# A running maximum taken in four chunks, transposes in one pass, and small operations moved between engines, in a fused adaLN, mLSTM and mixture-of-experts kernel

## The chip, the cores and the metric

The kernel runs on one core of a Trainium2 chip. The metric is the device time of one execution in microseconds, and several executions give a median. A second source is one profiled execution of the kernel, with a record for each instruction. The engines are TensorE (PE; PEld are its weight loads), VectorE (DVE), ScalarE (ACT), GpSimd (POOL) and SyncE (SP), which issues most transfers. All data is float32; fp32r is a float32 that TensorE multiplies in one pass.

## What is computed

For each of 8 rows of 512 tokens with 128 features: a layer norm with shift and scale from a small condition vector, an mLSTM block, a gated residual, a second layer norm, and a mixture of 8 experts with the best 2 of them.

```python
h = _layernorm(x) * (1 + ca) + sa
normed = h * rsqrt(mean(h * h) + 1e-6) * norm_w        # rms norm
q, k, v, zi, zf, o = projections of normed             # o through a sigmoid
# one step for each of the 512 tokens
m_t = maximum(zf_t + m, zi_t)
i_p = exp(zi_t - m_t);  f_p = exp(zf_t + m - m_t)
C_t = f_p * C + i_p * outer(v_t, k_t);  n_t = f_p * n + i_p * k_t
h_t = o_t * (C_t @ q_t) / maximum(abs(sum(n_t * q_t)), 1.0)
# then
x = x + ga * (h + h_t @ Wout.T)
h = _layernorm(x) * (1 + cb) + sb
gate = softmax over the best two of h @ Wr + br
x = x + gb * sum_e gate_e * (relu(h @ W1_e + b1_e) @ W2_e + b2_e)
```

The recurrence is computed for all tokens of a row at once. With F the running sum of zf and a = zi − F, the maximum of the recurrence is m_t = F_t + M_t with M the running maximum of a over the tokens. The weight of token s in the output of token t is exp(a_s − M_t) for s up to t, times the score k_s · q_t. So the kernel needs M along the tokens, and it needs it in every partition, since the weights stand with s on the partitions and t along the free dimension.

## The kernel before

A row of 512 tokens is NT = 4 tiles of P = 128 tokens. The code of each engine is one function, `body`, called for b = −2 to 7, in steps t = 3 to 18. A call, a *turn*, interleaves three rows. Row b is in its expert part: there are N = 16 steps, half an expert each. Row b + 1 ends its mLSTM part (`end`): output product, residual, second layer norm, logits, gates. Row b + 2 begins (`start`): first norm, projections, running sum and maximum, weights, products with v. The first turn (b = −2) has no expert part and no ending row. In the second (b = −1, `opening`) the expert part begins at step 16. From b = 0 to 5 all three rows are present. The turns for b = 6 and 7 have no starting row.

In an expert step t, PE makes three products of 512 columns for the first layer (L1109 to L1111: high part times high part and the two cross terms), and three for the second layer of step t − 3 (L1125, L1126, L1135). Between them DVE applies bias, relu and gate (hg, L852), ACT rounds to the high part (hg_hi, L521), and DVE or POOL subtracts to get the low part (hg_lo). `POOL_STEPS` says which steps are POOL's (L468): 1 and 8 to 15. The other low parts are DVE's (L865). The last product of step t − 3 waits for the low part. After its six products PE runs `chain(b, end, start, t)`, the small products of the other two rows. DVE has `middle(t)` ahead of a possible low part and `after(t)` behind it.

The order on every engine is written out by hand. Each engine takes its instructions in that order, and semaphores make it wait for the others. SP writes the gates of a row to DRAM and reads them back, spread over the partitions (gate_bc), and its queue goes in order too. The first hg of the next row waits for that transfer.

The steps that the change touches, in a turn with b from 0 to 5:

- Step 8: POOL takes rms from ms_eps by a power (L456), behind four operations of the second norm. Step 9: DVE waits for it and makes rms2, its square (L749), rms_inv, its reciprocal (L750), and copies rms to the last column of vs (L751). Then it makes zo, zg, the running sum zp (L806) and vs.
- Step 11: DVE makes a_col, 128 tokens on the partitions by 4 tiles (L816).
- Step 12: PE turns the four columns into one row of 512, four transposes into one partition (L1013), and makes the scores of tile 0 (L949, L950). DVE takes top_d and max_index for the gates of row b + 1 (L730, L732), and then the running maximum m_row over the 512 elements of the one partition (L820).
- Step 13: PE spreads m_row over 128 partitions, as ones times m_row, a full float32 product of two passes with one row of the array (L1024). DVE runs the chain to the gates (L737 to L785), then makes mb, the spread maximum with the triangle mask (L823).
- Step 14: PE transposes the gates (L1146), ACT copies them to gate_rows (L563), and SP writes them out. PE's first product of step 15 waits for gate_rows. Steps 14 to 16: ACT makes the weights ew from mb and a_col (L498, L500), DVE multiplies them with the scores (L700). Step 18: PE multiplies them with vs (L1039), and DVE makes the denominator den from rms_inv (L890) and uh.

## Time and profile before

| | us |
|---|---|
| median of 3 runs | 338.03 |
| lowest and highest | 336.07, 340.14 |
| the profiled execution | 336.87 |
| its span, first instruction to last | 335.0 |
| mean granted clock of PE | 0.995 |

The profiled execution's time is 1.87 us above its span. A turn is read as the distance from one L961 to the next. Durations are of that one execution. Products of PE are pipelined: the duration of one overlaps the next, so what one costs in PE's order is the distance from its start to the next start. "Idle before" in brackets is the time that the engine waited ahead of an instruction, with the instruction that released it.

### The profile page before, as it was taken

Reading aid. Unit: us, or ns where it says so; the run is one execution under the profiler, and the core shown is the slowest. Engines: PE = TensorE matmul, PEld = TensorE weight load, DVE = VectorE, ACT = ScalarE, POOL = GpSimd, SP = SyncE. Lnnn points to the kernel's source line nnn. Section 1 sums busy time; section 2 is a strip of 40 time slices with the busy share of each in tenths; the row PEclk is TensorE's granted clock in tenths of the full one; section 3 lists DMA queues with packets and bytes.
Section 4 is the critical chain, followed back from the end, with each engine's and each line's share of the span. In section 5 each row is a group of like instructions: output and inputs, shape, how many; then the busy total and the mean of one; then the engine's idle time right before and its main releaser. Section 6 shows DMA issues by size and latency. Waiting matters only on the chain.

```text
span 335.0 us, 5104 instructions
## 1 busy us (share of the span) xinstructions
PE 323.0 (96%) x1767; PEld 258.4 (77%) x1767; DVE 280.8 (84%) x800; ACT 165.7 (49%) x303; POOL 171.1 (51%) x173
## 2 busy tenths in 40 slices
PE   7989989999999999999999999999999989999996
PEld 7769756887787868786888778786878668777995
DVE  6796696999699987999699969998779958887874
ACT  1542426555546554563755564754547363346542
POOL 6440550588427853487347842785408832435440
PEclk9999999999999999999999999999999997999999
DMA  4770004100250006100520025000610034004201
GB/s 132 243 203 0 2 0 153 72 1 0 81 204 3 0 6 249 31 1 2 201 85 0 0 78 210 0 2 2 250 34 0 0 115 171 1 1 179 75 2 31
DMA packets 13456, 23.62 MB, mean 71 GB/s; under 512 B 1764, under 2 KB 8087, under 8 KB 12407
## 3 DMA queue, kind: packets, MB, share of 16 engines
q1 hardware_dynamic: 13202, 23.17, 20.4%
q8 instruction: 14, 0.23, 0.3%
q14 instruction: 12, 0.09, 0.1%
q10 hardware_dynamic: 164, 0.07, 0.1%
q0 software_dynamic: 64, 0.07, 0.1%
HBM read 21.07 MB, written 2.23 MB: 70 GB/s over the span
## 4 chain that ended last, share of the span: by engine, by line
PE 78%; DVE 8%; DMA 5%; POOL 3%; ACT 2%; issue 2%; SPq 1%; DVEq 0%; POOLq 0%
PE bank L1109 9%; PE bank L1125 8%; PE bank L1111 8%; PE bank L1110 8%; PE bank L1135 8%; PE bank L1126 8%; PE bank L1039 6%; PE bank L1024 3%; PE bank L972 3%; DMA gate_bc<-gates_d 2%; DMA br_bc<-in_L_ffn_br_dram 2%; PE bank L1154 2%; PE bank L987 2%; PE bank L1146 1%; PE bank L1160 1%
## 5 line engine op out<-in xcount | busy, mean ns | idle before, releaser
L468 POOL TENSOR_TENSOR hg_lo<-hg,hg_hi 128x512 fp32r<-128x512 f32 x65 | 87.7, 1358 | 73.7 <-ACT hg_hi L521 73.7
L521 ACT ACTIVATE hg_hi<-hg 128x512 fp32r<-128x512 f32 x128 | 79.8, 628 | 77.9 <-DVE hg L852 76.7
L852 DVE SCALAR_TENSOR_TENSOR hg<-bank,neg_b,gate_bc 128x512 f32<-128x512 f32 x128 | 94.2, 741 | 25.1 <-DMA gate_bc<-gates_d 14.0
L1109 PE MATMUL bank<-h_hi,w_hi 128*128 128x512 f32 x128 | 58.5, 457 | 1.5 <-ACT gate_rows L563 1.5
L1125 PE MATMUL bank<-hg_hi,w_hi 128*128 128x512 f32 (+1 forms) x144 | 53.8, 374 | 0.0
L1135 PE MATMUL bank<-hg_lo,w_hi 128*128 128x512 f32 (+1 forms) x144 | 53.4, 371 | 0.0
L1126 PE MATMUL bank<-hg_hi,w_lo 128*128 128x512 f32 (+1 forms) x144 | 53.1, 369 | 0.0
L1111 PE MATMUL bank<-h_lo,w_hi 128*128 128x512 f32 x128 | 50.8, 397 | 0.0
L1110 PE MATMUL bank<-h_hi,w_lo 128*128 128x512 f32 x128 | 50.7, 396 | 0.0
L865 DVE TENSOR_TENSOR hg_lo<-hg,hg_hi 128x512 fp32r<-128x512 f32 x63 | 47.4, 752 | 1.1 <-ACT hg_hi L521 0.6
L437 POOL TENSOR_SCALAR var_eps<-mv 128x4 f32<-128x4 f32 x16 | 4.0, 251 | 66.7 <-DVE mv L598 66.7
L1109 PEld LDWEIGHTS bank<-h_hi,w_hi 128*128 128x128 f32 x128 | 24.3, 190 | 12.5 <-DVE hg L852 8.9
L1126 PEld LDWEIGHTS bank<-hg_hi,w_lo 128*128 128x128 f32 x144 | 27.3, 190 | 5.5
L1125 PEld LDWEIGHTS bank<-hg_hi,w_hi 128*128 128x128 f32 x144 | 27.2, 189 | 5.6
L1135 PEld LDWEIGHTS bank<-hg_lo,w_hi 128*128 128x128 f32 x144 | 27.1, 188 | 5.5 <-DVE hg_lo L865 0.3
L1111 PEld LDWEIGHTS bank<-h_lo,w_hi 128*128 128x128 f32 x128 | 24.2, 189 | 5.8
L1110 PEld LDWEIGHTS bank<-h_hi,w_lo 128*128 128x128 f32 x128 | 24.4, 191 | 3.6 <-issue 1.4
L1039 PEld LDWEIGHTS bank<-vs,ew 128*128 128x128 f32 x160 | 18.6, 193 | 3.3 <-DVE ew L700 3.2
L700 DVE TENSOR_TENSOR ew<-ew,bank 128x512 f32<-128x512 f32 (+3 forms) x32 | 14.8, 482 | 7.0 <-ACT ew L500 6.7
L1039 PE MATMUL bank<-vs,ew 128*128 128x65 f32 x160 | 19.5, 277 | 1.2 <-DVE ew L700 1.1
L447 POOL TENSOR_TENSOR xn<-xn,rstd 128x512 f32<-128x512 f32 x16 | 18.1, 1129 | 2.6 <-POOL rstd L444 0.5
L444 POOL TENSOR_TENSOR rstd<-var_eps,minus_half 128x4 f32<-128x4 f32 x16 | 19.3, 1206 | 0.0
(168 smaller groups left out, 557.0 us busy)
## 6 DMA issues: line engine op xcount, KB each, us to landing
gate_bc<-gates_d SPq DMA_DIRECT2D x8, 1024.0 KB, 7.0
gate_bc<-gates_d SPq DMA_DIRECT2D x8, 512.0 KB, 5.0
gate_bc<-gates_d SPq DMA_DIRECT2D x14, 256.0 KB, 3.6
out_dram<-x_all SPq DMA_DIRECT2D x7, 256.0 KB, 2.3
w_raw<-in_L_ffn_W_dram SPq DMA_DIRECT2D x1, 1024.0 KB, 8.5
x_all<-in_L_attn_x_dram SPq DMA_DIRECT2D x2, 256.0 KB, 4.2
wmod_sb<-in_L_wmod_dram SPq DMA_DIRECT2D x1, 384.0 KB, 4.9
out_dram<-x_all SPq DMA_DIRECT2D x2, 128.0 KB, 1.9
```

Source lines behind the costliest of these rows:

```text
L444: g.tensor_tensor(rstd[k][:, :], var_eps[k][:, :], minus_half[:, :], ALU.pow).then_inc(s_rs[k], 1)
L468: g.tensor_tensor(hg_lo[k][:, :], hg[k][:, :], hg_hi[k][:, :].bitcast(fp32), ALU.subtract).then_inc(s_lo_pool, 1)
L521: a.activation(hg_hi[k][:, :], hg[k][:, :], ACT.Copy).then_inc(s_hghi, 1)
L852: v.scalar_tensor_tensor(hg[k][:, :], up_bank[n % 4][:, :], neg_b1[:, n:n + 1], gate_bc[own % 2][:, n // NU, :], ALU.max, ALU.mult).then_i ...
L865: v.tensor_tensor(hg_lo[k][:, :], hg[k][:, :], hg_hi[k][:, :].bitcast(fp32), ALU.subtract).then_inc(s_lo_dve, 1)
L1039: last = t_.matmul(bA[:, q * NS:(q + 1) * NS], ew[:, o:o + P], vs[:, j, :], start=j == 0, stop=j == q)
L1109: t_.matmul(dst, w_hi, hx, start=True, stop=False)
L1110: t_.matmul(dst, w_lo, hx, start=False, stop=False)
L1111: t_.matmul(dst, w_hi, hl, start=False, stop=True).then_inc(s_up, 1)
L1125: t_.matmul(y[:, c0:c1], w_hi, hg_hi[k][:, c0:c1], start=n == 0, stop=False)
L1126: t_.matmul(y[:, c0:c1], w_lo, hg_hi[k][:, c0:c1], start=False, stop=False)
L1135: last = t_.matmul(y[:, c0:c1], w_hi, hg_lo[k][:, c0:c1], start=False, stop=n == N - 1)
```

## The change

Five edits.

- PE transposes a_col, all four columns together, into four partitions (4x128) instead of one. DVE scans the four chunks at the same time, 4x128 (m_chunk), ahead of top_d in step 12. PE transposes m_chunk back to 128x4, and its last column, spread over 128 columns, so that every partition gets the maxima of the four chunks. DVE scans three of these four (m_before: the maximum of all chunks ahead of each chunk), and takes the maximum of both (m_col, 128x4).
- In step 13 PE spreads m_col by four transposes, the stationary operand of each being one column repeated 128 times, in place of the product ones times m_row.
- POOL's low part of step 12 waits for the gates of row b + 1 (s_gates), in turns that have an ending and a starting row.
- The square of rms moves from DVE to POOL, behind the power and ahead of the low part of step 8. The column of vs moves to ACT, in step 10 behind the tanh. The reciprocal moves to the end of DVE's turn, just ahead of den.
- A constant of 1x512 becomes one of 128x128; m_before's first column is set at the start.

DVE around steps 12 and 13 of a steady turn, before (L852 is hg):

```order
L852 SCALAR_TENSOR_TENSOR hg<-bank,neg_b,gate_bc 128x512
L730 TENSOR_TENSOR top_d<-mx 128x4
L732 MAX_INDEX ix<-mx,lg 128x8 x4
L820 SCALAR_TENSOR_TENSOR m_row<-bank,neg_row 1x512
L852 SCALAR_TENSOR_TENSOR hg<-bank,neg_b,gate_bc 128x512
L737 TENSOR_SCALAR top_s<-top_e 128x4
L739 TENSOR_TENSOR gate_a<-iota_e,ix 128x32
```

and now (L876 is hg, m_before and m_col are the two new small operations):

```order
L876 SCALAR_TENSOR_TENSOR hg<-bank,neg_b,gate_bc 128x512
L737 SCALAR_TENSOR_TENSOR m_chunk<-bank,neg 4x128
L753 TENSOR_TENSOR top_d<-mx 128x4
L755 MAX_INDEX ix<-mx,lg 128x8 x4
L841 SCALAR_TENSOR_TENSOR m_before<-bank,neg 128x3
L844 TENSOR_TENSOR m_col<-bank,m_before 128x4
L876 SCALAR_TENSOR_TENSOR hg<-bank,neg_b,gate_bc 128x512
L760 TENSOR_SCALAR top_s<-top_e 128x4
```

The scan over one partition has gone from behind max_index. A scan over four partitions stands ahead of top_d, and two operations over 128 partitions behind max_index.

PE from the transpose of a_col in step 12 to the start of step 14, in the same turn, before:

```order
L1013 MATMUL bank<-ident,a_col 1x128 x4
L949 MATMUL bank<-qq,kk 128x512
L950 MATMUL bank<-qz,kk 128x512
L1109 MATMUL bank<-h_hi,w_hi 128x512
L1110 MATMUL bank<-h_hi,w_lo 128x512
L1111 MATMUL bank<-h_lo,w_hi 128x512
L1125 MATMUL bank<-hg_hi,w_hi 128x512
L1126 MATMUL bank<-hg_hi,w_lo 128x512
L1135 MATMUL bank<-hg_lo,w_hi 128x512
L1024 MATMUL bank<-m_row,ones 128x512
```

and now:

```order
L1039 MATMUL bank<-ident,a_col 4x128
L976 MATMUL bank<-qq,kk 128x512
L977 MATMUL bank<-qz,kk 128x512
L1047 MATMUL bank<-ident,m_chunk 128x4
L1048 MATMUL bank<-ident,m_chunk 128x4
L1142 MATMUL bank<-h_hi,w_hi 128x512
L1143 MATMUL bank<-h_hi,w_lo 128x512
L1144 MATMUL bank<-h_lo,w_hi 128x512
L1158 MATMUL bank<-hg_hi,w_hi 128x512
L1159 MATMUL bank<-hg_hi,w_lo 128x512
L1168 MATMUL bank<-hg_lo,w_hi 128x512
L1055 MATMUL bank<-ident,m_col 128x128 x4
```

One transpose stands for four, two of four columns follow the scores, and four of 128 columns take the place of the product with m_row.

POOL from the power of step 8 to the end of the turn's low parts, with the semaphores that each instruction waits for, before:

```order
L456 TENSOR_TENSOR rms<-ms_eps,minus_half 128x4 [waits s_mse]
L468 TENSOR_TENSOR hg_lo<-hg,hg_hi 128x512 [waits s_hghi]
L463 TENSOR_TENSOR h_lo<-h2T,h_hi 128x512 [waits s_h2hi,s_h2]
L468 TENSOR_TENSOR hg_lo<-hg,hg_hi 128x512 [waits s_hghi] x8
L437 TENSOR_SCALAR var_eps<-mv 128x4 [waits s_mv0]
```

and now:

```order
L464 TENSOR_TENSOR rms<-ms_eps,minus_half 128x4 [waits s_mse]
L468 TENSOR_TENSOR rms<-rms 128x4 [waits s_v,s_rms]
L482 TENSOR_TENSOR hg_lo<-hg,hg_hi 128x512 [waits s_hghi]
L475 TENSOR_TENSOR h_lo<-h2T,h_hi 128x512 [waits s_h2hi,s_h2]
L482 TENSOR_TENSOR hg_lo<-hg,hg_hi 128x512 [waits s_hghi] x3
L482 TENSOR_TENSOR hg_lo<-hg,hg_hi 128x512 [waits s_hghi,s_gates]
L482 TENSOR_TENSOR hg_lo<-hg,hg_hi 128x512 [waits s_hghi] x4
```

The square is the second row, behind the power and ahead of step 8's low part. The low parts of steps 9 to 15 and of the next row's step 1 have the same places, and the one of step 12 has the second wait, s_gates.

The diff, without the lists of semaphores:

```diff
@@ -95,7 +95,7 @@
         far = sb("far", [P, P])
         mean_col = sb("mean_col", [P, 1])
-        neg_row = sb("neg_row", [1, T])
+        neg = sb("neg", [P, P])
         iota_e = sb("iota_e", [P, E])
         minus_half = sb("minus_half", [P, NT])
@@ -161,7 +161,9 @@
         th = sb("th", [P, NT, DH])
         a_col = sb("a_col", [P, NT])
-        m_row = sb("m_row", [1, T])
+        m_chunk = sb("m_chunk", [NT, P])
+        m_before = sb("m_before", [P, NT])
+        m_col = sb("m_col", [P, NT])
         mb = sb("mb", [P, NT, P])
         ew = sb("ew", [P, NW])
@@ -420,7 +428,7 @@
             g.memset(ones[:, :], 1.0).then_inc(s_const, 1)
             g.memset(mean_col[:, :], 1.0 / D).then_inc(s_const, 1)
-            g.memset(neg_row[:, :], -3e38).then_inc(s_const, 1)
+            g.memset(neg[:, :], -3e38).then_inc(s_const, 1)
             for e in range(E):
                 g.memset(iota_e[:, e:e + 1], float(e)).then_inc(s_const, 1)
@@ -454,6 +462,10 @@
                         pool.wait_ge(s_mse, m2 + 1)
                         g.tensor_tensor(rms[:, :], ms_eps[:, :], minus_half[:, :], ALU.pow).then_inc(s_rms, 1)
+                        pool.wait_ge(s_rms, m2 + 1)
+                        if m2 > 0:
+                            pool.wait_ge(s_v, m2)
+                        g.tensor_tensor(rms2[:, :], rms[:, :], rms[:, :], ALU.mult).then_inc(s_rms2, 1)
                     if t == (11 if opening else 9 if b == -2 else 5) and ahead:
                         norm(0, b + 3)
@@ -464,6 +476,8 @@
                         k = (t - 1) % 4
+                        if t - 1 == 12 and end and start:
+                            pool.wait_ge(s_gates, m1 + 1)
                         pool.wait_ge(s_hghi, b * N + t)
                         g.tensor_tensor(hg_lo[k][:, :], hg[k][:, :], hg_hi[k][:, :].bitcast(fp32), ALU.subtract).then_inc(s_lo_pool, 1)
@@ -550,6 +564,10 @@
                         act.wait_ge(s_zo, m2 + 1)
                         a.activation(th[:, :, :], zo[:, :, :], ACT.Tanh, scale=0.5).then_inc(s_th, 1)
+                    if t == 10 and start:
+
+                        act.wait_ge(s_rms, m2 + 1)
+                        a.activation(vs[:, :, DH], rms[:, :], ACT.Copy).then_inc(s_vcol, 1)
                     if t == 12 and end:
@@ -601,6 +619,7 @@
             v.memset(warm[:, :], 0.0).then_inc(s_warm, 1)
             v.memset(gates[:, :, :], 0.0).then_inc(s_gz, 1)
+            v.memset(m_before[:, 0:1], -3e38).then_inc(s_Mz, 1)
             v.memset(gateT[:, :].bitcast(fp32), 0.0).then_inc(s_zero, 1)
@@ -712,6 +731,10 @@
                 def middle(t):
+                    if start and t == 12:
+
+                        dve.wait_ge(s_aT, m2 + 1)
+                        v.tensor_tensor_scan(m_chunk[:, :], bA[0:NT, M0:M0 + P], neg[0:NT, :], -3e38, ALU.max, ALU.max).then_inc(s_Mc, 1)
                     if end:
                         if t == 3:
@@ -746,9 +769,6 @@
                         if t == 9:
                             dve.wait_ge(s_rms, m2 + 1)
-                            v.tensor_tensor(rms2[:, :], rms[:, :], rms[:, :], ALU.mult).then_inc(s_rms2, 1)
-                            v.reciprocal(rms_inv[:, :], rms[:, :])
-                            v.tensor_copy(vs[:, :, DH], rms[:, :])
                     if ahead and t == 4:
                         norm_stats(0, b + 3)
@@ -816,8 +836,12 @@
                         if t == (13 if opening else 12):
-                            dve.wait_ge(s_aT, m2 + 1)
-                            v.tensor_tensor_scan(m_row[0:1, :], bA[0:1, :], neg_row[0:1, :], -3e38, ALU.max, ALU.max).then_inc(s_M, 1)
+                            dve.wait_ge(s_McT, m2 + 1)
+                            dve.wait_ge(s_Mz, 1)
+                            v.tensor_tensor_scan(m_before[:, 1:NT], bA[:, M1 + NT:M1 + 2 * NT - 1], neg[:, 0:NT - 1], -3e38,
+                                                 ALU.max, ALU.max).then_inc(s_Mp, 1)
+                            dve.wait_ge(s_Mp, m2 + 1)
+                            v.tensor_tensor(m_col[:, :], bA[:, M1:M1 + NT], m_before[:, :], ALU.max).then_inc(s_M, 1)
                         if t == 13:
                             dve.wait_ge(s_Mb, m2 + 1)
@@ -886,6 +910,8 @@
                 if start:
+                    v.reciprocal(rms_inv[:, :], rms[:, :]).then_inc(s_rinv, 1)
+                    dve.wait_ge(s_rinv, m2 + 1)
                     dve.wait_ge(s_pv, m2 + 1)
                     v.tensor_tensor(den[:, :], pv[:, :, DH], rms_inv[:, :], ALU.max).then_inc(s_den, 1)
@@ -896,7 +922,8 @@
                     out_rows(b)
-            F0 = 8
+            F0, M0 = 8, 2 * NVO + 8
+            M1 = M0 + P
             gates3 = gates[:, :, :].rearrange("p j (c w) -> p j c w", c=3)[:, :, :, 0:E]
             pv = bA[:, 0:NT * NS].rearrange("p (j n) -> p j n", j=NT)
@@ -1009,19 +1036,24 @@
                     if t == 12:
                         pe.wait_ge(s_a, m2 + 1)
-                        for j in range(NT):
-                            last = t_.transpose(bA[0:1, j * P:(j + 1) * P], a_col[:, j:j + 1], ident[:, :])
-                        last.then_inc(s_aT, 1)
+                        t_.transpose(bA[0:NT, M0:M0 + P], a_col[:, :], ident[:, :]).then_inc(s_aT, 1)
                         if end:
...
                         pe.wait_ge(s_qz, m2 + 1)
                         scores(0, bC[:, 0:T])
+
+                        pe.wait_ge(s_Mc, m2 + 1)
+                        t_.transpose(bA[:, M1:M1 + NT], m_chunk[:, :], ident[0:NT, 0:NT])
+                        t_.transpose(bA[:, M1 + NT:M1 + 2 * NT], m_chunk[:, P - 1:P].to_broadcast([NT, P]),
+                                     ident[0:NT, 0:NT]).then_inc(s_McT, 1)
                     if t == 13:
                         pe.wait_ge(s_zo, m2 + 1)
                         pe.wait_ge(s_M, m2 + 1)
-                        t_.matmul(bB[:, :], ones[0:1, :], m_row[0:1, :], start=True, stop=True).then_inc(s_Mb, 1)
+                        for j in range(NT):
+                            last = t_.transpose(bB[:, j * P:(j + 1) * P], m_col[:, j:j + 1].to_broadcast([P, P]), ident[:, :])
+                        last.then_inc(s_Mb, 1)
                     if t == 14:
@@ -1033,6 +1065,7 @@
                         pe.wait_ge(s_P, m2 * NT + NT)
+                        pe.wait_ge(s_vcol, m2 + 1)
                         for q in range(NT):
                             for j in range(q + 1):
@@ -1174,7 +1207,8 @@
                     y_transposes(b)
-            F0 = 8
+            F0, M0 = 8, 2 * NVO + 8
+            M1 = M0 + P
             body(-2, False, True, True, lambda n: False, first=True)
             pe.wait_ge(s_bc, 80)
             pe.wait_ge(s_zero, 1)
```

## Rows read from the trace of the kernel before

**Rows 1.** The page, parts 1 and 2: TensorE's busy share; its granted clock.

```profile
PE 323.0 (96%) x1767; PEld 258.4 (77%) x1767; DVE 280.8 (84%) x800; ACT 165.7 (49%) x303; POOL 171.1 (51%) x173
...
PEclk9999999999999999999999999999999997999999
```

**Rows 2.** Stretches: us, busy time (instructions) by engine, clock, DMA share, GB/s.

```profile
135.31:171.66 36.35, 36.05 (x195) 28.89 (x194) 32.43 (x94) 19.70 (x37) 21.86 (x19) 1.00 0.19 66
244.65:281.00 36.35, 35.13 (x184) 28.08 (x183) 29.09 (x81) 19.07 (x36) 18.12 (x15) 0.96 0.16 59
```

**Rows 3.** Timeline, PE, steps 12 to 15: start, us, engine, line, op, tiles, count.

```profile
116.51 0.60 PE L1013 MATMUL bank<-ident,a_col 128*1 128x128 f32 x4
116.86 0.48 PE L949 MATMUL bank<-qq,kk 128*128 128x512 f32 x1
...
117.41 0.40 PE L1109 MATMUL bank<-h_hi,w_hi 128*128 128x512 f32 x1
...
118.34 0.40 PE L1126 MATMUL bank<-hg_hi,w_lo 128*128 128x512 f32 x1
118.57 0.39 PE L1135 MATMUL bank<-hg_lo,w_hi 128*128 128x512 f32 x1
119.00 1.09 PE L1024 MATMUL bank<-m_row,ones 1*128 1x512 f32 x2
120.02 0.50 PE L1109 MATMUL bank<-h_hi,w_hi 128*128 128x512 f32 x1
...
121.29 0.40 PE L1135 MATMUL bank<-hg_lo,w_hi 128*128 128x512 f32 x1
121.70 0.63 PE L1146 MATMUL bank<-ident,gates 128*72 128x128 f32 x4
...
123.11 0.47 PE L1109 MATMUL bank<-h_hi,w_hi 128*128 128x512 f32 x1 [0.26 <-ACT gate_rows L563]
```

**Rows 4.** Timeline, DVE, steps 9 to 14 of the same turn.

```profile
110.76 1.24 DVE L749 TENSOR_TENSOR rms<-rms 128x4 f32<-128x4 f32 x1 [0.24 <-POOL rms L456]
...
116.27 0.74 DVE L852 SCALAR_TENSOR_TENSOR hg<-bank,neg_b,gate_bc 128x512 f32<-128x512 f32 x1
116.93 0.25 DVE L730 TENSOR_TENSOR top_d<-mx 128x4 f32<-128x4 f32 x1
...
117.66 1.19 DVE L820 TENSOR_TENSOR_SCAN m_row<-bank,neg_row 1x512 f32<-1x512 f32 x1
118.78 0.71 DVE L852 SCALAR_TENSOR_TENSOR hg<-bank,neg_b,gate_bc 128x512 f32<-128x512 f32 x1
...
120.40 1.25 DVE L785 TENSOR_TENSOR gates<-gate_a,gate_b 128x96 f32<-128x96 f32 x1
```

**Rows 5.** Timeline, POOL, the same stretch.

```profile
110.70 1.29 POOL L468 TENSOR_TENSOR hg_lo<-hg,hg_hi 128x512 fp32r<-128x512 f32 x1
...
115.87 3.77 POOL L468 TENSOR_TENSOR hg_lo<-hg,hg_hi 128x512 fp32r<-128x512 f32 x3 [0.59 <-ACT hg_hi L521]
120.24 1.30 POOL L468 TENSOR_TENSOR hg_lo<-hg,hg_hi 128x512 fp32r<-128x512 f32 x1 [0.60 <-ACT hg_hi L521]
```

**Rows 6.** By source line, over the whole run: nanoseconds, shortest, median, longest.

```profile
L749 DVE TENSOR_TENSOR rms<-rms x8: 162/1241/1248, 17.4 to 256.9; 128x4 f32<-128x4 f32 x8
...
L806 DVE TENSOR_TENSOR_SCAN zp<-ones,zg x8: 164/624/644, 19.0 to 259.6; 128x3 f32<-128x3 f32 x8
...
L785 DVE TENSOR_TENSOR gates<-gate_a,gate_b x8: 257/1236/1245, 49.9 to 300.6; 128x96 f32<-128x96 f32 x8
```

**Rows 7.** Timeline, PE, the opening turn.

```profile
51.40 1.09 PE L1024 MATMUL bank<-m_row,ones 1*128 1x512 f32 x2
```

**Rows 8.** Timeline, DVE and PE, the end of one turn.

```profile
274.90 0.75 DVE L852 SCALAR_TENSOR_TENSOR hg<-bank,neg_b,gate_bc 128x512 f32<-128x512 f32 x1 [3.18 <-DMA gate_bc<-gates_d]
...
276.23 0.55 PE L1039 MATMUL bank<-vs,ew 128*128 128x65 f32 x3 [0.91 <-DVE ew L700]
```

**Rows 9.** Timeline, weight loads of PE, the stretch of rows 3.

```profile
120.02 0.19 PEld L1109 LDWEIGHTS bank<-h_hi,w_hi 128*128 128x128 f32 x1 [0.76 <-DVE hg L852]
```

More of the change, by code:

```diff
@@ L248, in adaln_mlstm_moe_kernel @@
         s_rms2 = sem("s_rms2")
+        s_rinv = sem("s_rinv")
+        s_vcol = sem("s_vcol")
         s_vz = sem("s_vz")
@@ L257, in adaln_mlstm_moe_kernel @@
         s_aT = sem("s_aT")
+        s_Mc = sem("s_Mc")
+        s_McT = sem("s_McT")
+        s_Mz = sem("s_Mz")
+        s_Mp = sem("s_Mp")
         s_M = sem("s_M")
```

## The prediction

> **What bounds the kernel now.** I read the page's busy shares first, then the stretches by turn, then the three engines around steps 12 to 14 of one turn, and last the end of the turn. TensorE (PE) is busy for 96% of the span and its granted clock is full nearly everywhere [rows 1]. A turn of the steady part lasts 36.35 us, of which PE is busy for 36.05, while VectorE (DVE) has 3.9 us to spare, GpSimd (POOL) 14.5 and ScalarE (ACT) 16.7 [rows 2]. So work counts when it stands in PE's row, or when it makes PE wait. The row of PE around steps 12 to 15 holds both kinds [rows 3]: four transposes of a_col take 0.35 us of its order (116.51 to 116.86), and the product that spreads m_row takes 1.02 (119.00 to 120.02). A product of 512 columns takes 0.23 in this stream (118.34 to 118.57), so after the last one of step 13, at 118.57, the 119.00 leaves 0.20 over: PE waits for the running maximum. Between 121.29 and 121.70 the same sum leaves 0.18: PE waits for the gates. The gates' transposes start at 121.70 and the first product of step 15, which waits for the gate rows that ACT copies, at 123.11: 1.41 later, less than 0.3 of it PE's wait.
>
> The gates are late because of DVE [rows 4]. Its op that writes them lasts 1.25 us, and at the shortest of eight 0.257 [rows 6]. It ends just after a low part of POOL that started at 120.24 and took 1.30 [rows 5]. The square of rms is the same case: 1.24 at 110.76, ending 0.01 after POOL's low part of 110.70; its shortest of eight is 0.162 [rows 4 to 6]. Even top_d (0.25) ends at 117.18 and looks caught. The scan over m_row has one operand in PSUM, runs across POOL's ops and keeps to 1.19 [rows 4]. The Trainium skill, "SBUF — State Buffer", section "SBUF: two separate sides", says the same of the shared port pair: an exclusive lock for the whole instruction, which the loser waits out. By that rule, the trace agrees, with 1.24 against 0.162 us.
>
> **The change, part by part, in a steady turn.** Times are on the axis of rows 3 to 5.
>
> *Square, reciprocal, column.* DVE loses the 1.24 at 110.76 and two short ops behind it. POOL gets the square: 128x4 elements, at least the 0.15 of DVE's free one and at most the 1.24 of its blocked one; I take 0.25, the nearer end, since nothing there holds the port. The low part behind it starts that much later and its product is due two steps on: cost nothing; with 1.24 it would be about 1 us of POOL's spare 14.5. ACT gets a copy of four columns, hidden in its 16.7. The reciprocal at the turn's end delays den, uh and the output rows by some 0.2 us on DVE, hidden while DVE reaches the following two steps before PE needs them; uncovered it would cost 0.2. This gain on DVE is worth nothing to PE directly: hg(12) starts at 116.27, since the products of step 12 end about there. It lets a_col, and POOL's low parts 10 and 11, come up to 0.6 earlier.
>
> *One transpose for a_col.* Four take 0.35, so one takes 0.09: PE gains 0.26, but a wait follows at once.
>
> *Chunk scan.* It now stands ahead of top_d. a_col's transpose lands near 116.8 (four last 0.60 and start 0.09 apart, so one lasts 0.33) and hg(12) lets DVE go at 116.93, so it starts there and DVE hardly waits. Price: the scan of 512 took 1.19, one of three elements 0.164 at the shortest [rows 4, 6], so 2.0 ns an element, and 128 take 0.42 (bounds 0.16 and 1.19): done 117.35. PE has passed scores(0) at 117.41 − 0.26 = 117.15 by then and waits, then does two transposes of four columns. Their slot is bounded by 0.09 (one of the a_col transposes) and 0.5 (half of the 1.02 of m_row's two passes, the only row here with few partitions in the array); I take 0.25. Step 13 starts at 117.65, not 117.41: 0.24 lost.
>
> *Running maximum.* top_d and max_index took 0.73 (116.93 to 117.66). top_d is now asked for at 117.35, inside POOL's low part 11, the second of the three that run together from 115.87. That part would end at 118.38 if POOL came no earlier; with the earlier hg(10) and hg(11) I take 117.9. So 0.55 of lock (bounds 0 and 1.1), and max_index ends near 118.6. The scan of three and a maximum over 128x4, as short as the free square, add 0.164 + 0.162 and a handoff, 0.4 in all: s_M near 119.0, where it came at 118.85 before. The gain of the shorter scan is eaten by its place. hg(13) follows near 118.95, 0.17 later.
>
> *Spreading.* Six products at 0.23 are 1.39. PE arrives at 117.65 + 1.39 = 119.04, waits nearly nothing, and does four transposes, 0.35 by the a_col ones and a little for the full load. Step 14 starts at 119.5, not 120.02, and ends 1.50 later as before (121.29 + 0.23 − 120.02): 121.0.
>
> *Low part of step 12 behind the gates.* POOL is idle from low part 11 to the gates; the gates lose 0.99 of lock: they start at 120.40 + 0.17 = 120.57 and end at 120.83. So PE starts their transposes at 121.0 rather than 121.70, a **gain of 0.7**, to which I add 0.05 for its smaller wait on the gate rows: 0.75. POOL then runs low parts 12 and 13 from 120.8 to 123.4 (1.30 each). PE wants part 12 with the last product of step 15, about 122.4 + 1.2 = 123.6, 1.5 us after it is there. Uncovered, a step would wait up to 1.3.
>
> The gates' way through DRAM starts with the gate rows, so the next row's first hg moves along with PE, and the turn keeps the 0.75. With all bounds against it (lock 1.1, slot 0.5) step 14 starts at 119.9 and the gain is 0.3; with all for it (no lock, slot 0.1) it is 1.0.
>
> **Sum.** Six steady turns (L749 runs eight times [rows 6]; two are the opening ones): 6 × 0.75 = 4.5. In the opening turn the maximum is spread at 51.40 by the same product [rows 7]. Four transposes there save 1.02 − 0.38 = 0.64, the scan's 1.19 shrinks to 0.4 behind the gates, but the chunk scan pushes the gates back 0.4: I take 0.8 (0.3 to 1.1). In the first turn the maximum waits behind other work on DVE: 0.1. Together 5.4, against the profiled 336.87: 331.5. The runs shown have their median 1.16 above the profiled one; on it the sum gives 332.6. I forecast **332.0**.
>
> **Rivals.**
> *Handoffs eat it.* If the chunk scan costs like the whole one (1.19), DVE is done at 118.1, step 13 starts at 118.4, step 14 at 120.2, and PE is at the gates at 121.7: nothing gained per turn, 0.5 in all, 336.4. For it: three round trips between PE and DVE where two were. Against: the three-element scan of 0.164.
> *The DRAM way becomes the wait.* In one turn DVE stood idle for 3.18 us until the gates were back, PE for 0.91 behind it, and that turn's mean clock is 0.96 [rows 2, 8]. The other steady turn has 36.35 − 36.05 = 0.30 of idle PE in all. If every turn ended with 0.6 more, six would give back 3.6: 335.1 by the profiled time, 336.2 by the median. Against: both sides of that race start at the gate rows and move together.
> *Slower.* Here the transposes don't overlap their loads. A load of 128 columns takes 0.19 [rows 9] and one transpose lasts 0.33, so six in a row, two for the chunks and four for the columns, take 6 × 0.52 = 3.1. PE would be at 117.35 + 3.1 + 1.39 + 1.50 = 123.3 at the gates instead of 121.70: 1.6 lost per turn, 6 × 1.6 = 9.6, 346.5. It decides from the point where the six take over 1.46 together (121.70 − 117.35 − 1.39 − 1.50). For it stand the few rows of the chunk's stationary, and the 1.02 that m_row's two passes take where two products take 0.46. Against it: four a_col transposes with four loads fit in 0.35. The Trainium skill, "TensorE: Matmul & The Clock Gate", section "Part 3: Packing small matmuls", says that loads overlap running matmuls only when the row group differs. By that rule this rival would hold; the 0.35 speaks against it.
> *More than summed.* No lock on top_d and no fall of the clock at the end: 6 × 1.0 + 1.1, and 1 for the clock, of the 0.04 × 36.35 = 1.5 at most: 328.8.
> That the change does not free the gates of the lock would need another POOL op there; it has none until s_gates.
>
> **Chances.** Forecast 0.62 (329.9 to 334.7 by the bounds), more than summed 0.06, handoffs 0.13, DRAM way 0.10, slower 0.09. The range 328.5 to 336.5 leaves out the slower case, about half of the two near 336, and a little below. A measurement tells about 1% from no change: faster means under 334.65, slower over 341.4. Faster 0.68 (forecast and more), same 0.23 (the two near 336), slower 0.09.
>
> **What would show it.** The gates' op at 0.26 in all eight turns; the chunk scan near 0.42; top_d stretched to 0.5 or more; 1.15 from the a_col transpose to step 13; the four column transposes within 0.4; a steady turn of 35.6. I am wrong if PE stands idle before the chunk transposes for more than 0.8, if the low part of step 12 is what PE waits for in step 15, or if the turn's end takes up a wait that the middle gave.

## The result, and the profile after

The changed kernel takes 327.7 us (median of 4 runs, 327.37 to 330.12), the one before, run beside it, 337.62 (4 runs). The ratio is 0.973, 95% interval 0.969 to 0.977: faster by 2.7%. I had forecast 332.0 with a range from 328.5. The sign was right; the time lies 0.8 below the range. The profiled execution took 327.37 (span 325.6), against 336.87 (span 335.0) before, and is told here.

The page, parts 1 and 2, as [rows 1]:

```profile
PE 314.3 (97%) x1775; PEld 257.9 (79%) x1775; DVE 264.2 (81%) x801; ACT 166.0 (51%) x311; POOL 171.5 (53%) x181
...
PEclk9999999999999999999999999999999999999999
```

DVE lost 16.6 us of busy time and PE 8.7, and the 7 in PE's clock row is gone. By stretch (columns as in [rows 2]), a steady turn and the one that answers to 244.65:281.00:

```profile
132.29:167.85 35.56, 35.24 (x195) 29.00 (x194) 30.03 (x94) 19.70 (x38) 22.00 (x20) 1.00 0.20 67
239.03:274.39 35.36, 35.08 (x195) 29.00 (x194) 28.64 (x86) 19.79 (x38) 18.11 (x16) 1.00 0.20 68
```

The steady turn is 0.79 shorter. Outside its busy time PE has 0.32 in it, 0.30 before. The gain lies in work that PE no longer does and in short waits that the overlapping durations of its products hide (0.20 and 0.18 before, by the starts in [rows 3]).

PE's timeline, the turn that answers to [rows 3]. Its first instruction after the turn's start (transposes of h_ga) is at 96.59, at 98.34 before, so 1.75 is added to compare:

```profile
113.77 0.39 PE L1144 MATMUL bank<-h_lo,w_hi 128*128 128x512 f32 x1
...
114.69 0.28 PE L1039 MATMUL bank<-ident,a_col 128*4 128x128 f32 x1
...
115.04 0.40 PE L977 MATMUL bank<-qz,kk 128*128 128x512 f32 x1
115.47 0.22 PE L1047 MATMUL bank<-ident,m_chunk 4*128 4x4 f32 x1
115.55 0.19 PE L1048 MATMUL bank<-ident,m_chunk 4*128 4x4 f32 x1
115.67 0.50 PE L1142 MATMUL bank<-h_hi,w_hi 128*128 128x512 f32 x1
...
117.17 0.60 PE L1055 MATMUL bank<-ident,m_col 128*128 128x128 f32 x4
117.53 0.48 PE L1142 MATMUL bank<-h_hi,w_hi 128*128 128x512 f32 x1
...
119.00 0.60 PE L1179 MATMUL bank<-ident,gates 128*72 128x128 f32 x4
...
120.37 0.47 PE L1142 MATMUL bank<-h_hi,w_hi 128*128 128x512 f32 x1 [0.25 <-ACT gate_rows L581]
```

Step 13's first product (115.67, so 117.42) comes 0.01 later than before, step 14's (117.53, so 119.28) 0.74 earlier, the gates' transposes (119.00, so 120.75) 0.95 earlier and step 15 (120.37, so 122.12) 0.99. The four transposes of m_col take 0.36 of PE's order, the two of m_chunk 0.20, where the product ones times m_row took 1.02. These distances repeat: from the turn's start to step 15 it is 24.76 to 24.80 in all six steady turns before, and 23.78 to 23.81 in all six after.

DVE, answering to [rows 4]:

```profile
114.20 0.75 DVE L876 SCALAR_TENSOR_TENSOR hg<-bank,neg_b,gate_bc 128x512 f32<-128x512 f32 x1 [0.60 <-PE bank L1144]
115.00 0.41 DVE L737 TENSOR_TENSOR_SCAN m_chunk<-bank,neg 4x128 f32<-4x128 f32 x1
115.34 0.67 DVE L753 TENSOR_TENSOR top_d<-mx 128x4 f32<-128x4 f32 x1
...
116.49 0.13 DVE L841 TENSOR_TENSOR_SCAN m_before<-bank,neg 128x3 f32<-128x3 f32 x1
116.66 0.16 DVE L844 TENSOR_TENSOR m_col<-bank,m_before 128x4 f32<-128x4 f32 x1
...
118.30 0.26 DVE L805 TENSOR_TENSOR gates<-gate_a,gate_b 128x96 f32<-128x96 f32 x1
```

POOL, answering to [rows 5]:

```profile
109.05 0.20 POOL L468 TENSOR_TENSOR rms<-rms 128x4 f32<-128x4 f32 x1
...
112.25 3.74 POOL L482 TENSOR_TENSOR hg_lo<-hg,hg_hi 128x512 fp32r<-128x512 f32 x3
118.64 2.53 POOL L482 TENSOR_TENSOR hg_lo<-hg,hg_hi 128x512 fp32r<-128x512 f32 x2 [2.65 <-DVE gates L805]
```

POOL stands idle for 2.65 until the gates are there, and DVE writes them in 0.26 in place of 1.25. By source line (columns as in [rows 6]):

```profile
L805 DVE TENSOR_TENSOR gates<-gate_a,gate_b x8: 257/258/261, 50.5 to 291.4; 128x96 f32<-128x96 f32 x8
...
L737 DVE TENSOR_TENSOR_SCAN m_chunk<-bank,neg x8: 404/411/411, 21.7 to 257.4; 4x128 f32<-4x128 f32 x8
...
L753 DVE TENSOR_TENSOR top_d<-mx x8: 166/670/693, 48.7 to 289.8; 128x4 f32<-128x4 f32 x8
```

**Where 9.4 us of the span went.** The turns start at (first the opening turn, then six steady ones, then the end of the sixth):

```text
before   32.05   62.03   98.34  135.15  171.49  207.85  244.49  283.56
after    32.00   61.33   96.59  132.29  167.85  203.42  239.03  274.39
```

Up to the first steady turn the change gains 0.70, over five steady turns 4.76, in the sixth 3.71, and behind it 0.23. The five give 0.95 each, but unevenly. Up to step 15 every turn gains 0.98 or 0.99. What follows step 15 varies from turn to turn by some tenths in both kernels (11.5 to 12.1 us in these five turns before, 11.5 to 11.9 after), and between the medians, 36.36 and 35.57, the gain is 0.79. In the sixth, the gates' return from DRAM was late before [rows 8], and the clock fell behind it (columns as in [rows 2]; clock third from the end; kernel before):

```profile
277.00:278.00 1.00, 1.00 (x11) 1.00 (x10) 0.97 (x2) 1.00 (x2) 0.43 (x1) 1.00 1.03 430
278.00:279.00 1.00, 1.00 (x9) 1.00 (x8) 1.00 (x3) 0.11 (x2) 1.00 (x1) 0.65 0.97 410
279.00:280.00 1.00, 1.00 (x6) 0.90 (x5) 0.71 (x4) 0.59 (x1) 0.40 (x1) 0.50 0.34 139
280.00:281.00 1.00, 1.00 (x4) 0.80 (x3) 0.47 (x1) 0.00 (x0) 0.00 (x0) 0.50 0.00 0
```

At 0.50 (the 1.2 GHz level) 4 to 6 of PE's instructions fall into one us, at full clock 11. Two more profiled executions of the kernel before (337.46 and 336.16 us) had the late return without the fall: their sixth turns took 37.44 and 37.41. So the 39.07 of the forecast's trace holds some 1.65 of clock and 1.05 of late return over a turn of 36.35. Both are absent after: of the sixth turn's 3.71, 2.7 is this and 1.0 the turn's own gain.

The clock can be taken out of the comparison altogether. Of the executions whose mean granted clock was 0.998 or more, the kernel before has 18 of 81 (the 81 that ran beside the experiments), with a median of 334.9, and the changed kernel 7 of 10, with a median of 327.4. At full clock the change is worth 7.5 us.

### The profile page after: what moved, and what is told of

Same layout as the page of the kernel before. It is cut to its first block, busy times and chain, and to the rows that moved or that the text cites. A ratio compares the mean times of both kernels' runs of the same rounds, so it can differ in the third digit from the quotient of the medians.

```text
span 325.6 us, 5182 instructions
## 1 busy us (share of the span) xinstructions
PE 314.3 (97%) x1775; PEld 257.9 (79%) x1775; DVE 264.2 (81%) x801; ACT 166.0 (51%) x311; POOL 171.5 (53%) x181
## 4 chain that ended last, share of the span: by engine, by line
PE 79%; DVE 8%; DMA 6%; ACT 2%; issue 2%; SPq 1%; POOL 1%; DVEq 0%; POOLq 0%
PE bank L1142 9%; PE bank L1144 8%; PE bank L1168 8%; PE bank L1158 8%; PE bank L1143 8%; PE bank L1159 8%; PE bank L1072 6%; DMA gate_bc<-gates_d 3%; PE bank L999 3%; PE bank L1187 2%; PE bank L1014 2%; PE bank L1019 2%; DMA br_bc<-in_L_ffn_br_dram 2%; PE bank L1193 1%; DMA gates_d<-gate_rows 1%
## 5 line engine op out<-in xcount | busy, mean ns | idle before, releaser
L876 DVE SCALAR_TENSOR_TENSOR hg<-bank,neg_b,gate_bc 128x512 f32<-128x512 f32 x128 | 94.3, 743 | 25.5 <-DMA gate_bc<-gates_d 13.2
L1158 PE MATMUL bank<-hg_hi,w_hi 128*128 128x512 f32 (+1 forms) x144 | 53.1, 369 | 0.0
```

The source lines that it names most:

```text
L876: v.scalar_tensor_tensor(hg[k][:, :], up_bank[n % 4][:, :], neg_b1[:, n:n + 1], gate_bc[own % 2][:, n // NU, :], ALU.max, ALU.mult).then_i ...
L1158: t_.matmul(y[:, c0:c1], w_hi, hg_hi[k][:, c0:c1], start=n == 0, stop=False)
```

## The experiments

Call the parts **S** (square to POOL, column to ACT, reciprocal late), **M** (the whole maximum: one-pass a_col, chunk scans, transposes) and **G** (POOL's wait for the gates). The table holds all kernels. "To 15" is the distance from the turn's start to step 15, the median of the six steady turns of the profiled execution; they differ by 0.05 at most. "Turn" is the median of its first five steady turns; these differ by some tenths. "Full" counts the executions with a mean granted clock of 0.998 or more. The ratio is to the kernel before in the same batch of runs.

```
kernel      parts or edit            median us (n)  ratio [95%]           to 15  turn   full
before      four batches together    336.4 (81)                           24.77  36.36  18 of 81
g_only      G                        335.52 (10)    0.995 [0.991, 0.999]  24.57  36.24  0 of 10
s_only      S                        339.98 (10)    1.009 [1.004, 1.014]  25.40  37.03  2 of 10
m_only      M                        338.76 (10)    1.005 [1.000, 1.010]  25.55  37.14  1 of 10
gs          G, S                     337.58 (10)    1.005 [1.001, 1.008]  25.18  36.77  5 of 10
sm          S, M                     334.92 (11)    0.997 [0.993, 1.001]  24.94  36.56  2 of 11
gm          G, M                     330.07 (4)     0.976 [0.970, 0.982]  24.24  35.83  3 of 4
after_again G, S, M (the change)     327.38 (6)     0.973 [0.968, 0.978]  23.80  35.58  4 of 6
fill_end    before + fillers         336.73 (12)    1.005 [1.001, 1.009]  24.79  36.41  4 of 12
idle_end    change + DVE idles PE    331.27 (6)     0.985 [0.980, 0.990]  23.79  35.81  0 of 6
row1        change + 1-row prod.     335.07 (12)    0.998 [0.994, 1.001]  24.99  36.56  5 of 12
row128      change + 128-row prod.   333.52 (6)     0.990 [0.986, 0.993]  24.66  36.45  1 of 6
mct_late    change, transposes moved 326.62 (6)     0.970 [0.967, 0.973]  23.68  35.32  6 of 6
best        mct_late + b2_split      325.04 (6)     0.969 [0.965, 0.972]  23.68  35.26  6 of 6
```

**G alone.** The kernel before with the wait added:

```diff
                         k = (t - 1) % 4
+                        if t - 1 == 12 and end and start:
+                            pool.wait_ge(s_gates, m1 + 1)
                         pool.wait_ge(s_hghi, b * N + t)
```

> The kernel before, with the second wait of POOL's low part of step 12 alone. Theory (two limits meet at the gates' transposes, PE's own order and the gates, and the later one counts): the gates' op falls from 1.24 to 0.26 us, the gates are there 1 us earlier, but PE's order keeps the spreading product and reaches the transposes at 121.52 instead of 121.70 of the old axis: 0.2 us per steady turn, 1.1 in all. Rival (each part brings its own gain, and the sum of the parts is the whole): the lock is the largest part, 0.5 per turn or more, 3 us in all.

Step 15 comes 0.20 earlier in every turn, and the ratio is 0.995. That is the theory's 0.2: with the gates free, PE's own order is the later of the two.

**S alone.**

```diff
+                        g.tensor_tensor(rms2[:, :], rms[:, :], rms[:, :], ALU.mult).then_inc(s_rms2, 1)
...
+                        a.activation(vs[:, :, DH], rms[:, :], ACT.Copy).then_inc(s_vcol, 1)
...
-                            v.tensor_tensor(rms2[:, :], rms[:, :], rms[:, :], ALU.mult).then_inc(s_rms2, 1)
-                            v.reciprocal(rms_inv[:, :], rms[:, :])
-                            v.tensor_copy(vs[:, :, DH], rms[:, :])
...
+                    v.reciprocal(rms_inv[:, :], rms[:, :]).then_inc(s_rinv, 1)
```

> The kernel before, with only the square on POOL, the column on ACT and the reciprocal at the turn's end. Theory: VectorE stands 1.2 us earlier in step 9 and has lost it again at step 12, where it waits for PE's products, so a steady turn gains 0 to 0.2 us. Rival (VectorE sets the turn and every microsecond it loses counts): 1.2 per turn, 7 us in all.

From rms to vs DVE needs 1.48 where it needed 3.24, and yet step 15 comes 0.63 later. Neither theory nor rival had a loss. DVE, POOL and PE of s_only, step 12 to 14:

```profile
118.59 1.15 DVE L740 TENSOR_TENSOR top_d<-mx 128x4 f32<-128x4 f32 x1
...
115.95 3.76 POOL L474 TENSOR_TENSOR hg_lo<-hg,hg_hi 128x512 fp32r<-128x512 f32 x3
...
121.56 1.09 PE L1033 MATMUL bank<-m_row,ones 1*128 1x512 f32 x2 [0.68 <-DVE m_row L827]
```

POOL's three low parts end at 119.71. DVE comes to top_d when the third of them has just begun, and top_d ends at 119.74. It took 0.25 in [rows 4], where DVE came to it 0.25 later in the turn, just before one of POOL's low parts ended. The lock that the square had has moved to top_d, and there it stands in the chain to m_row: PE waits 0.68 where 0.20 was left over before.

**M alone.** The change without the hunks of G and S:

> The kernel before, with only the running maximum in chunks and the one-pass transposes. Theory: PE's order is shorter by 0.7 us up to the gates' transposes, but the gates' op still waits out a low part of POOL, so PE waits for it there: 0 to 0.2 us per steady turn, and the idle time moves in front of the gates' transposes. Rival (PE is the bound and work taken off it counts in full): 0.7 per turn, 4 to 5 us in all.

Step 15 comes 0.78 later, where a gain of 0 to 0.2 was expected. DVE, POOL and PE of m_only, steps 12 to 14:

```profile
154.61 1.17 DVE L741 TENSOR_TENSOR top_d<-mx 128x4 f32<-128x4 f32 x1
157.17 0.77 DVE L748 TENSOR_SCALAR top_s<-top_e 128x4 f32<-128x4 f32 x1
158.25 1.04 DVE L791 TENSOR_TENSOR top_g<-top_g,top_e 128x4 f32<-128x4 f32 x1
...
153.23 2.54 POOL L474 TENSOR_TENSOR hg_lo<-hg,hg_hi 128x512 fp32r<-128x512 f32 x2 [0.59 <-ACT hg_hi L527]
156.62 2.65 POOL L474 TENSOR_TENSOR hg_lo<-hg,hg_hi 128x512 fp32r<-128x512 f32 x2 [0.86 <-ACT hg_hi L527]
...
159.87 0.52 PE L1167 MATMUL bank<-ident,gates 128*72 128x128 f32 x3 [1.11 <-DVE gates L796]
```

POOL's low parts end at 155.77, 157.91 (the first of its second pair) and 159.27; top_d, top_s and top_g end at 155.78, 157.94 and 159.29. Three small ops each wait out a low part, PE's own row is shorter, and PE stands idle for 1.11 before the gates. The op that writes the gates is itself free here, 0.26. The Trainium skill, "SBUF — State Buffer", section "SBUF: two separate sides", has the loser of the shared port wait for the whole instruction; the three pairs of ends, 0.01 to 0.03 apart, agree.

**The pairs.** gm, gs and sm each leave one part out of the change.

> The chunked maximum and the second wait of POOL together, with square, column and reciprocal where they were before. Theory: both limits fall together, 0.7 to 0.9 us per steady turn, well over the sum of the two alone. With square and the rest still on VectorE, the chunk scan may start 0.3 later. Rival (the parts add up): the sum of g_only and m_only.

> The kernel before with the second wait of POOL and the moved square, column and reciprocal, without the chunked maximum: the last corner of the eight. Theory (a lock is a matter of meeting: the moved square shifts POOL's low parts and lets top_d run into low part 11, 0.7 us per turn, seen in s_only; the gates are free by the wait): s_only's 37.02 less what the freed gates give while PE's order keeps the spreading product, 36.2 to 36.6 per turn. Rival (with the gates free nothing of the lock is left on the way): 36.15 or less, as g_only.

> The kernel after, without the second wait of POOL's low part of step 12. Theory: the gates' op is back at 1.24 us and PE waits for the gates, so 0.7 us or more of the 0.95 per steady turn is lost again, 4 to 6 us slower than after. Rival (VectorE comes early enough by the moved square to miss the lock): the same time as after.

Up to step 15, against 24.77: S +0.63, M +0.78, G −0.20, GS +0.41, SM +0.17, GM −0.53, GSM −0.99. S and M each harm alone and hurt less together than either. G turns M from +0.78 to −0.53. S on top of G and M brings 0.46 more. In gs top_d still lasts 1.12, which is S's harm with free gates. The single effects add up to +1.21, the change gives −0.99. Three expectations missed in size: gm had 0.7 to 0.9 and gained 0.53, gs had a turn of 36.2 to 36.6 and took 36.77, and sm had 4 to 6 us over the changed kernel and took 7.5.

Whole times hold one thing more than the first 25 us of a turn. sm's median is below that of the kernel before, although it comes to step 15 later. Its sixth turn took 36.67 and not 37.4, as the late return is nearly gone there too, and the opening turn gains 0.6 with M (29.98 before, 29.32 in m_only, 29.35 in gm).

What S brings on top of G and M is seen in gm, which lacks only S (its turn starts at 97.23, the one shown of the change at 96.59, so 0.64 is taken off to compare):

```profile
115.12 0.75 DVE L869 SCALAR_TENSOR_TENSOR hg<-bank,neg_b,gate_bc 128x512 f32<-128x512 f32 x1
115.78 0.40 DVE L727 TENSOR_TENSOR_SCAN m_chunk<-bank,neg 4x128 f32<-4x128 f32 x1
116.11 1.17 DVE L743 TENSOR_TENSOR top_d<-mx 128x4 f32<-128x4 f32 x1
...
118.24 0.62 PE L1046 MATMUL bank<-ident,m_col 128*128 128x128 f32 x4
...
120.09 0.60 PE L1169 MATMUL bank<-ident,gates 128*72 128x128 f32 x4
```

Without S, hg(12) starts with no idle time ahead of it, at 114.48 against 114.20, and the chunk scan at 115.14 against 115.00. top_d then falls almost whole into a low part of POOL (1.17 against 0.67), the transposes of m_col start at 117.60 against 117.17, and those of the gates at 119.45 against 119.00.

**The change again**, beside these:

> The kernel after once more, for its clock over more executions and beside the next three. Theory: most executions keep the full clock from end to end, 327.4 to 327.8, and the rest lose 1.5 to 3 us to a stretch at half clock. Rival (the falls are chance and as frequent as before): a full clock in about 1 execution of 5, and a median near 329 to 330.

327.38 and 0.973, as the first time. 4 of 6 kept the full clock, 326.53 to 327.81, and the other two took 328.13 and 331.12.

**Is it the clock?** fill_end gives the kernel before two filler products ahead of the wait that ends the sixth turn, so that PE idles less there:

```diff
+                        if b == B - 3:
+                            pe.wait_ge(s_E, m2 * NT + NT)
+                            for _ in range(2):
+                                t_.matmul(bB[:, :], ident[:, :], w1_raw[:, 0:2, :].rearrange("p e f -> p (e f)"),
+                                          start=True, stop=True)
                         pe.wait_ge(s_P, m2 * NT + NT)
```

> The kernel before, with two filler products (about 0.9 us of PE) ahead of the last products of the sixth steady turn, where the trace of before had PE idle for about 1.1 us and the granted clock at 0.5 from 3 us later on. The fillers' result is not used. Theory (the idle stretch brings the clock down): the turn's clock stays at 1.00 in most runs and the kernel is 1.5 to 2 us faster than before although it does more. Rival (the fall has nothing to do with that idle stretch): the fall stays, and the time is the same or up to 0.9 longer.

The theory's gain of 1.5 to 2 us did not come: the ratio is 1.005. 4 of 12 kept the full clock, against 18 of 81, which is too close to tell a difference. The profiled execution kept it, and its sixth turn took 38.05. idle_end makes PE idle at that place in the change:

```diff
+                            if b == B - 3:
+                                v.memset(scratch[:, 0:1024], 0.0)
                             scores_times_weights(m2, 3)
```

> The kernel after, with one write of 128x1024 zeros (0.9 us) to an unused buffer on VectorE ahead of the last two weights of the sixth steady turn, so that PE stands idle for 0.9 us longer there. Theory: the granted clock falls in that place in most runs, and the kernel is 0.9 + 1.7 = 2.6 us slower than after. Rival: the clock stays, 0.9 us slower.

None of 6 kept it, and the ratio rose to 0.985. But the profiled execution does not lay this to the forced idle time. Its two stretches at 0.5 begin at 11 and 48 us, long before the edit does anything. At the forced place PE idled for 0.97 and the clock stayed, as it did in the third steady turn, where the gates came late by themselves:

```profile
167.96 0.77 PE L1075 MATMUL bank<-vs,ew 128*128 128x65 f32 x5 [1.82 <-DVE ew L720]
...
275.64 2.45 PE L1075 MATMUL bank<-vs,ew 128*128 128x65 f32 x20 [0.97 <-DVE ew L720]
```

So the count differs from the changed kernel's 7 of 10, and nothing shows why.

**Does a product of one row cost clock?** The kernel before has one in each turn, the change has none. row1 puts an unused one into the change, row128 one of 128 rows:

```diff
                         pe.wait_ge(s_zo, m2 + 1)
+                        if 0 <= b:
+                            t_.matmul(bB[:, :], ones[0:1, :], w1_raw[0:1, 0:2, :].rearrange("p e f -> p (e f)"),
+                                      start=True, stop=True)
```

> The kernel after with an unused product of one row of the array by 512 columns in step 13 of every steady turn, like the one that spread m_row before. Both theories: about 1.0 us per turn, 6 in all, by its place in PE's order. Theory on the clock (a product that keeps one row of the array busy counts as idle for it): the falls come back, a full clock in at most 1 execution of 4. Rival: the clock is as in the kernel after.

> As the run with one row, with all 128 rows in the unused product. Both theories: 0.9 us per turn, 5 to 5.5 in all. Theory on the clock: full as in the kernel after, and so more than 0.1 per turn faster than the one with one row. Rival: no difference to it beyond the 0.1 to 0.2 per turn of the product itself.

The theory had at most 1 in 4 at full clock with one row, and with 128 rows as many as in the change. It came out the other way round, 5 of 12 and 1 of 6. So few executions refute nothing, but the theory has nothing left for it. The price in PE's order is clear: step 15 comes 1.20 later with one row and 0.87 later with 128 (1.0 and 0.9 expected).

**A shorter wait for the chunks.** In the change PE idles 0.2 between scores(0) and the chunk transposes (115.27 to 115.47). mct_late puts these behind step 13's first three products:

```diff
-                        pe.wait_ge(s_Mc, m2 + 1)
-                        t_.transpose(bA[:, M1:M1 + NT], m_chunk[:, :], ident[0:NT, 0:NT])
...
+                    if t == 13 and start:
+                        pe.wait_ge(s_Mc, b + 3)
+                        t_.transpose(bA[:, M1:M1 + NT], m_chunk[:, :], ident[0:NT, 0:NT])
```

> The kernel after with the two transposes of m_chunk issued behind the first three products of step 13 in place of ahead of them. Theory: PE's idle 0.2 us before them goes, s_M is not later since VectorE is at max_index then, and a steady turn is 0.2 to 0.3 us shorter, 1.2 to 1.8 in all (326.0). Rival (the gates or the gate rows' way through DRAM are already the bound): the 0.2 comes back as a wait at the gates' transposes or ahead of step 15, the same time.

Step 13 starts 0.40 earlier in the turn, but step 15 only 0.11 to 0.12. The 0.2 of idle time is gone, and the two transposes cost more inside the stream of products: from the third product (116.04) to the fourth (116.58) it is 0.54, where two products in a row stand 0.23 apart, and from the fourth to the fifth (116.91) it is 0.33. Over the six turns the mean falls by 0.20, the median time by 0.8, to 326.62, short of the 1.2 to 1.8 expected.

**A version that beats both.** best adds the move of b2_split, in the opening turn, from DVE's step 10 to POOL's step 14:

```diff
+                    if opening and t == 14:
+                        pool.wait_ge(s_mask, m2 + 1)
+                        g.memset(b2_parts3[:, :].bitcast(fp32), 0.0).then_inc(s_b2z, 1)
...
-                    if opening and t == 10:
-                        b2_split()
```

> The kernel with the later chunk transposes, and the splitting of b2 in the opening turn moved from VectorE, where it stood ahead of a_col (2.7 us), to POOL behind the mask. Theory: a_col of the opening turn is there 1.5 us earlier, PE's idle 1.24 ahead of it goes, and 0.5 to 1.5 us are gained of 326.6, less where POOL's norm locks the chain to the gates. On the clock: if the idle stretch at 48 us is what lets it fall there, it falls no more. Rival: the gates wait for POOL's norm anyway, and the time stays within 0.3.

325.04, where mct_late, in another batch, took 326.62. PE in the opening turn, of the change:

```profile
48.01 0.27 PE L1039 MATMUL bank<-ident,a_col 128*4 128x128 f32 x1 [1.24 <-DVE a_col L836]
...
50.82 0.63 PE L1179 MATMUL bank<-ident,gates 128*72 128x128 f32 x4
```

and of best:

```profile
45.73 0.27 PE L1037 MATMUL bank<-ident,a_col 128*4 128x128 f32 x1
...
49.09 0.63 PE L1177 MATMUL bank<-ident,gates 128*72 128x128 f32 x4 [0.40 <-DVE gates L805]
```

PE's 1.24 of idle time before a_col are gone. Of the 1.73 by which the gates' transposes stand earlier, 0.89 was there at the turn's start (31.11 against 32.00), before the edit acts; the edit gives 0.84, and the opening turn is 0.83 shorter (28.50 against 29.33). The ratios of mct_late and best, 0.970 and 0.969, don't tell the two apart, so what stands on this edit is the 0.83 of the trace. Five of best's six executions (325.78 or less) are faster than all ten of the change (326.53 or more). mct_late's range, 326.38 to 327.51, overlaps the change's.

## Why the prediction was wrong, step by step

Right in mechanism and size:
- **Low part behind the gates.** The gates' op at 0.258 in all eight, 0.26 expected. POOL had the time: PE never waits for low part 12.
- **Square on POOL** 0.20 (0.25 taken), hidden, like the copy on ACT.
- **Chunk scan** 0.41 (0.42), **lock on top_d** 0.50 over its free 0.17 (0.55), **spreading** 0.36 (within 0.4), chunk transposes' slot 0.20 (0.25).
- **The slower rival** (transposes that don't overlap their loads, 3.1 for six) is out: the four take 0.36 together and the two start 0.08 apart. The rule of the Trainium skill, "TensorE: Matmul & The Clock Gate", section "Part 3: Packing small matmuls", by which loads overlap only when the row group differs, does not hold for these.
- **Handoffs** and **the DRAM way** are out too: idle PE before the chunk transposes is 0.2, and of the 0.99 that step 15 gains the five turns keep 0.95 on average. Between the medians it is 0.79, so 0.2 is given back behind step 15 there. That the median turn came out at the 35.6 of the forecast is luck: the 0.99 was larger than the 0.75 forecast, and the 0.2 was not in it.

Failed:
1. **"This gain on DVE is worth nothing to PE directly: hg(12) starts at 116.27, since the products of step 12 end about there."** This is the step that failed. It took a start that DVE set for one that PE set. In the kernel before, DVE runs without a pause from a_col into hg(12), and the product that hg(12) needs had started at 115.58:

```profile
115.58 0.39 PE L1111 MATMUL bank<-h_lo,w_hi 128*128 128x512 f32 x1
...
116.21 0.14 DVE L816 TENSOR_TENSOR a_col<-zg,bank 128x4 f32<-128x4 f32 x1
```

After, the same product starts at 113.77 and hg(12) at 114.20, 0.43 behind it, and now it is DVE that waits for PE (0.60); before, hg(12) started 0.69 behind it. [rows 4] hold the sign: no idle time stands ahead of hg at 116.27. So hg(12) came at 115.95 of the old axis, 0.32 earlier than the sum had it, of which 0.07 is PE's own row. The chunk scan follows (116.75 for 116.93), step 13 (117.42 for 117.65), step 14 (119.28 for 119.5) and the gates' transposes (120.75 for 121.0). The price of this step is measured: gm has no S, and reaches the gates' transposes 0.45 later in the turn than the change. The sum gave the square's move nothing and the whole middle 0.7; the middle gained 0.95, near the 1.0 that it had as the best case. In the sum the six turns stand at 4.5 and measured 5.8 (4.76 and 1.0).
2. **The end of the sixth turn, priced at nothing in the forecast.** It is only in the rival "more than summed", at 1, with a chance of 0.06. The late return and the clock fall were worth 1.05 and 1.65, 2.7 together. Without them the profiled time would have been 330.1, inside the range. The error was one of baseline: the trace of before, on which the sum stood, had a fall at that place that other executions do not have (two more traces have none there, and 18 of 81 executions have none at all), and I let it stay in the changed kernel. The trace of the change has none.
3. **The opening**: 0.70 in place of 0.8 and 0.1 for the first turn, within its bounds.

The sum of 5.4, with 1.3 more for the six turns, 2.7 for the end of the sixth, 0.2 less for the opening and 0.2 behind the turns, gives the 9.4 measured.

What the single edits show beside that: the gain that the sum gives to "low part behind the gates" and to "spreading" belongs to neither alone. With the order of M but without G, the 0.5 that PE's shorter row saves in gm turns into 1.11 of waiting. I had called the chain by its parts, and each of the sum's terms holds only in the presence of the others.

**Left open.** Why the clock falls more seldom after the change (7 of 10 executions keep it full, 18 of 81 before). The falls last 3 to 7 us at 0.5. In 17 profiled executions they stood ahead of the first steady turn or near a turn's end, mostly behind idle PE, as here in the kernel before (another execution), where PE's clock falls in the us in which it has no work:

```profile
46.00:47.00 1.00, 0.78 (x2) 0.00 (x0) 0.96 (x2) 0.00 (x0) 1.00 (x2) 1.00 0.00 0
47.00:48.00 1.00, 0.00 (x0) 0.00 (x0) 0.94 (x8) 0.00 (x0) 0.87 (x1) 0.89 0.00 0
48.00:49.00 1.00, 0.99 (x5) 0.73 (x6) 1.00 (x11) 0.20 (x1) 0.99 (x1) 0.50 0.00 0
```

The same idle time is in every kernel but best, and most of the changed kernel's executions keep the clock through it; m_only idles 1.1 in every turn without a fall in them. Idle PE stood ahead of most falls and doesn't decide them. Why the sixth turn's gate reads are late is open too. SP takes 3.53 us to issue the four in the kernel before (3.47 and 3.44 in its two other traces), 1.98 after and 1.75 in most other turns. In g_only it takes 3.28 and in gs 2.90, in s_only 1.75, and 2.53 or less in all kernels with M. So it changed with the edits, but no run tried it apart.

## What to carry to other kernels

A small VectorE op on SBUF alone costs either its own time or the rest of a GpSimd instruction. Taking such a blocked op out moves the lock to the next one, so ask which op will be asked for inside GpSimd's next run and whether PE waits for it; edits of this kind are to be judged together. An instruction with no idle time ahead of it is late by its own engine: before another engine's work is called its start, look at when that work was done. And before a sum is made against one profiled execution, read its turns side by side: a turn that stands out by 2.7 us is a term of its own, and whether the change keeps it needs a price and a chance.

## What the runs showed of the hardware beyond what was expected

- The lock also catches a TENSOR_SCALAR of 128x4 (top_s 0.77 in m_only, 0.15 at the shortest) and a scan whose operands are both in SBUF (zp, 0.62 in [rows 6], 0.164 at the shortest and in the changed kernel). The scans with a bank as operand kept their time across POOL's low parts (m_chunk 0.404 to 0.411 in all eight).
- Transposes of four partitions start 0.08 apart (115.47 and 115.55), with a load each.
- A product of one row by 512 columns costs more of PE's order than one of 128 rows: 1.20 and 0.87 in the same place (row1, row128).
- SP's issue of the same four DMAs can take 3.53 us in one turn and 1.75 in the others.
